# Four graph layers on one core: half-steps of a Householder reduction moved between the low halves of a software pipeline

## The chip, the core and the metric

One core of a Trainium2 chip runs the whole program as one launch. The metric is the device time in microseconds of that core, as the median of 3 runs. The engines are TensorE (PE), VectorE (DVE), ScalarE (ACT), GpSimd (POOL) and SyncE (SP), which issues the loads and stores here.

## What is computed

Four residual layers over x of shape (128, 64, 256), each `x = layernorm(x + layer(x))`. The change lies in the first one and in a small matrix job for the last one:

```python
# layer 0: two graph convolutions, then four window LSTMs (p = 1..4)
h = relu(einsum('ts,bsh->bth', adj, x @ Wg0 + bg0))
h = relu(einsum('ts,bsh->bth', adj, h @ Wg1 + bg1))
for p in range(1, 5):
    wins = h[:, :nw * p, :].reshape(Bv * nw, p, Hd)
    last = lstm_last(Wih[p-1], Whh[p-1], bih[p-1], bhh[p-1], wins)
    h = h.at[:, arange(nw) * p + (p - 1), :].set(last)
...
# layer 3: eigenvectors of the normalized 64 x 64 graph Laplacian
_, U = eigh(L_norm)
out = U @ ((U.T @ x) @ W1 ...) @ W2 ...
```

All products are made from two parts, a high half rounded to the matmul type and a low half that is the rest, with three matmuls for one (high by high, high by low, low by high: lines 473 to 475). ScalarE makes the high halves, VectorE the low ones.

## The kernel before

The 8192 rows are worked in 16 groups of 512. `graph_layers` runs them through a software pipeline of turns (`for it in range(...)`, 19 turns from 0 to 18), written out by hand for each engine; engines meet only by semaphores. In turn `it` TensorE's queue holds: `project_input(it)` (x times Wg0, 28 matmuls), `project_output(it - 2)` (times Wg1), the LSTM products of window length 1 for the second half of group `it - 3`, `mix_to_features(it - 1)` (adjacency, 24 matmuls), `mix_rows(it)` (adjacency, 6 matmuls), and the LSTM products for the first half of group `it - 2`. Products of one half are 18 matmuls of 128x512.

The results go through three pairs of PSUM banks: `pair_a` holds the projected input (`ps_y`) and the mixed features (`ps_ax`), `pair_b` the first layer and the output, `pair_c` is used by group 1's projected input alone, in turn 1; from turn 2 on its banks are part of the LSTM's ring of four.

VectorE's queue in a common turn (3 to 15) is: `hidden` of the LSTM (`hT`, L1977, waits for ScalarE's tanh), a reflection, `projected_low` (`y_lo`, L1565), `input_low` (`xs_lo`, L1561), `rows_low` (`l_x_lo`, L1910, twice), `cell` (`l_cell`, L1970), a second reflection, `mixed_low` (`ax_lo`, L1573), `first_low` (`h_lo`, L1569), `hidden`, `cell`.

A reflection is one of 62 steps of the Householder reduction of the Laplacian to tridiagonal form, on 32 partitions. Step k has three parts on VectorE: `back_products` (L206 to L214, waits for GpSimd's `scaled`), `back_update` (L222 to L231) and `front` of step k + 1 (L174 to L180). GpSimd does `basis` (L244, L246) after the update and `scalars` (L189 to L197) after the front; L196 releases the next `back_products`. So the reflections are a chain between VectorE and GpSimd that runs beside the graph stage. `REFLECTION_AT` says which halves of which turns hold one: both halves of turns 2 to 15 and the first half of 16, 29 in all. The other 33 are done in the LSTM stage of window lengths 2 and 3.

A pipeline turn's dependencies that matter here: `project_input(g)` waits for `xs_lo` of g and, from group 2 on, for `ax_lo` of g - 2 (same banks); `mix_to_features(g)` waits for `h_lo` of g and `y_lo` of g + 1 (the banks of `ps_y` are overwritten); `mix_rows(g)` for `y_lo` of g; `project_output(g)` for `ax_lo` of g and `h_lo` of g + 1; the LSTM's first-half products for `l_x_lo`.

SyncE issues the loads at the start: x of group 0, the adjacency twice in both orientations (block diagonal), Wg0, Wg1, the biases, then x of the further groups and the LSTM's first weights. `l_w1x_lo` (L1618) is the low half of those weights, in turn 1.

## Time and profile before

| | us |
|---|---|
| median of 3 runs | 2044.53 |
| lowest, highest | 2042.39, 2045.41 |
| the profiled execution | 2044.89 |
| its span in the trace | 2043.1 |
| graph stage and first LSTM, to the first product of window length 2 | 344.84 |
| turn 3's first product, turn 16's first | 55.87, 310.47 |

In the timeline a row is the start, the duration, the engine and line, what it writes and reads, and in brackets the idle time of the engine before it with what ended it.

### The profile page before, as it was taken

Reading aid. Unit: us, or ns where it says so; the run is one execution under the profiler, and the core shown is the slowest. Engines: PE = TensorE matmul, PEld = TensorE weight load, DVE = VectorE, ACT = ScalarE, POOL = GpSimd, SP = SyncE. Lnnn points to the kernel's source line nnn.
Section 4 is the critical chain, followed back from the end, with each engine's and each line's share of the span. In section 5 each row is a group of like instructions: output and inputs, shape, how many; then the busy total and the mean of one; then the engine's idle time right before and its main releaser. Section 6 shows DMA issues by size and latency. Waiting matters only on the chain. (4 is left out here: it accounts for less than half of the span.)

```text
span 2043.1 us, 32231 instructions
## 1 busy us (share of the span) xinstructions
PE 1915.3 (94%) x11545; PEld 1616.9 (79%) x11545; DVE 1519.5 (74%) x4011; ACT 1152.8 (56%) x1803; POOL 712.2 (35%) x1676
## 2 busy tenths in 40 slices
PE   6999999999999999999999989989699899689996
PEld 5888887888899999987887778867599434479895
DVE  6888786657566777888888879868565588789575
ACT  3555556445445454544344367657576688557575
POOL 2566651233233341000000056466543000108675
PEclk8999999999999999999999989989799999899898
DMA  3010101001000000010000043113212000003022
GB/s 115 22 32 22 52 1 42 1 1 42 1 1 1 1 1 1 1 42 1 1 1 1 1 150 104 63 38 97 73 65 71 1 1 1 11 30 128 22 73 83
DMA packets 61534, 71.13 MB, mean 35 GB/s; under 512 B 3767, under 2 KB 55102, under 8 KB 61374
## 3 DMA queue, kind: packets, MB, share of 16 engines
q1 hardware_dynamic: 61374, 69.07, 10.4%
q8 instruction: 91, 1.49, 0.3%
q14 instruction: 69, 0.57, 0.1%
HBM read 43.90 MB, written 25.17 MB: 34 GB/s over the span
## 5 line engine op out<-in xcount | busy, mean ns | idle before, releaser
L2002 ACT ACTIVATE l_gates<-l_acc,l_b 128x512 f32<-128x512 f32 (+1 forms) x408 | 240.7, 620 | 88.3 <-PE l_acc L475 86.3
L1900 ACT ACTIVATE l_x_hi<-hT 128x512 fp32r<-128x512 f32 (+1 forms) x144 | 101.2, 754 | 171.4 <-PE l_acc L475 170.9
L473 PE MATMUL l_acc<-l_x_hi,l_w1x_hi 128*128 128x336 f32 (+1 forms) x544 | 187.9, 345 | 4.0 <-ACT l_gates L2002 2.7
L475 PE MATMUL l_acc<-l_x_lo,l_w1x_hi 128*128 128x336 f32 (+1 forms) x544 | 188.3, 346 | 0.0
L474 PE MATMUL l_acc<-l_x_hi,l_w1x_lo 128*128 128x336 f32 (+1 forms) x544 | 188.3, 346 | 0.0
L473 PE MATMUL l_acc<-l_x_hi,l_w0x_hi 128*128 128x512 f32 x464 | 182.2, 393 | 5.4 <-ACT l_gates L2002 4.5
L475 PE MATMUL l_acc<-l_x_lo,l_w0x_hi 128*128 128x512 f32 x464 | 181.5, 391 | 0.0
L474 PE MATMUL l_acc<-l_x_hi,l_w0x_lo 128*128 128x512 f32 x464 | 181.3, 391 | 0.0
L2009 ACT ACTIVATE l_gates<-l_cell 128x512 f32<-128x512 f32 (+1 forms) x112 | 63.8, 569 | 191.2 <-DVE l_cell L2061 155.7
L244 POOL TENSOR_TENSOR bi_shifted<-bi_shifted 32x126 f32<-32x126 f32 (+61 forms) x62 | 17.7, 286 | 378.2 <-DVE bi_shifted L231 378.2
L1247 ACT ACTIVATE leaky<-sc_g 128x1024 f32<-128x1024 f32 x128 | 121.2, 1032 | 21.7 <-PE sc_g L1361 21.4
L473 PE MATMUL l_acc<-l_h_hi,l_w0h_hi 128*128 128x512 f32 x320 | 124.9, 390 | 4.4 <-DVE l_h_lo L2073 4.4
L2189 POOL TENSOR_TENSOR n_tmp<-n_stats 128x4 f32<-128x4 f32 x64 | 13.3, 208 | 329.2 <-DVE n_stats L2177 328.1
L475 PE MATMUL l_acc<-l_h_lo,l_w0h_hi 128*128 128x512 f32 x320 | 124.7, 390 | 0.0
L474 PE MATMUL l_acc<-l_h_hi,l_w0h_lo 128*128 128x512 f32 x320 | 124.7, 390 | 0.0
L473 PEld LDWEIGHTS l_acc<-l_x_hi,l_w1x_hi 128*128 128x128 f32 x544 | 103.3, 190 | 13.3 <-ACT l_gates L2002 3.2
L2206 ACT ACTIVATE hT<-hT,n_shift,n_rstd 128x256 f32<-128x256 f32 x192 | 99.4, 591 | 21.4 <-POOL n_shift L2201 21.4
L474 PEld LDWEIGHTS l_acc<-l_x_hi,l_w1x_lo 128*128 128x128 f32 x544 | 103.0, 189 | 8.6
L475 PEld LDWEIGHTS l_acc<-l_x_lo,l_w1x_hi 128*128 128x128 f32 x544 | 102.9, 189 | 8.7
L473 PEld LDWEIGHTS l_acc<-l_x_hi,l_w0x_hi 128*128 128x128 f32 x464 | 87.6, 189 | 25.5 <-ACT l_gates L2002 6.1
L2058 DVE TENSOR_TENSOR l_gates<-l_gates 128x512 f32<-128x512 f32 (+1 forms) x72 | 43.9, 610 | 80.6 <-ACT l_gates L2002 79.0
L475 PEld LDWEIGHTS l_acc<-l_x_lo,l_w0x_hi 128*128 128x128 f32 x464 | 87.4, 188 | 18.3
(519 smaller groups left out, 6231.3 us busy)
## 6 DMA issues: line engine op xcount, KB each, us to landing
xin<-in_x_t SPq DMA_DIRECT2D x16, 512.0 KB, 3.7
hidB<-in_x SPq DMA_DIRECT2D x16, 512.0 KB, 4.8
x<-hT SPq DMA_DIRECT2D x16, 512.0 KB, 3.2
hidB<-x SPq DMA_DIRECT2D x16, 512.0 KB, 3.8
x<-hidB SPq DMA_DIRECT2D x16, 512.0 KB, 2.9
attention_residual<-x SPq DMA_DIRECT2D x16, 512.0 KB, 3.9
out_x<-hT SPq DMA_DIRECT2D x16, 512.0 KB, 2.9
l_rawx<-in_wih SPq DMA_DIRECT2D x4, 1024.0 KB, 5.4
```

Of the source, the lines that this page charges most:

```text
L244: s.after(g.tensor_tensor(prod, vb[:, lo:].unsqueeze(1).to_broadcast([self.Q, 2, w]), self.p[k % 2][:, 2:4].unsqueeze(2).to_broadcast([sel ...
L473: t.matmul(out, left[0], right[0], start=start, stop=False)
L474: t.matmul(out, left[1], right[0], start=False, stop=False)
L475: return t.matmul(out, left[0], right[1], start=False, stop=stop)
L1247: a.activation(leaky[b % RING][:, :, :], ps_g[b % GATHERS][:, :, :], ACT.Prelu, alpha=SLOPE).then_inc(leaked, 1)
L1900: i = nc.scalar.activation(as_windows(xs[s % 2][0][:, ch, 0:bg * nw], nw), cols(p, bg, nw, group, k, ch), ACT.Copy)
L2002: i = a.activation(gates[:, j, q, 0:n], acc[:, j, q, 0:n], FUNC[q], bias=b[:, o:o + 1])
L2009: a.activation(tcell[:, j, 0:n], cell[:, j, 0:n], TANH).then_inc(tc, 1)
L2058: v.tensor_tensor(i_, i_, g_, ALU.mult)
L2189: s.add(p.tensor_tensor(apart, even[:, :, 1], odd[:, :, 1], ALU.subtract))
L2206: i = a.activation(rows[:, r, :], rows[:, r, :], ACT.Identity, bias=self.shift[:, g, r:r + 1], scale=self.rstd[:, g, r:r + 1])
```

## The change

- Loads: Wg0 is issued second, right behind x of group 0; Wg1 goes behind the biases. Each has a semaphore of its own, and ScalarE waits for each where it copies it.
- Start of TensorE: `project_input(0)` waits only for Wg0's low half, and for the bias's low half ahead of its first bias product.
- Banks: group 2's projected input goes to `pair_c` too, so `project_input(2)` waits for `y_lo` of group 1, and `mix_to_features(1)` no longer waits for `y_lo` of group 2.
- Reflections: in turn 2 there is only one, behind `input_low(3)` and ahead of `rows_low(0)`. In the common turns the second one is split: `mixed_low` stands between its products and its update with the next front. In turn 16 the one reflection moves from the first half to the second, behind `rows_low(14)`. 28 in all, so 34 are left to the LSTM stage.
- The wait for all reads of the ring moves from ahead of window length 2's products to their second half (`j == 1`), whose banks they are.

```diff
--- before.py
+++ after.py
@@ -478,7 +478,7 @@
 BIAS_ROWS = 96
 BEHIND = 3
 
-REFLECTION_AT = {at: k for k, at in enumerate([(it, half) for it in range(2, 16) for half in range(2)] + [(16, 0)])}
+REFLECTION_AT = {at: k for k, at in enumerate([(2, 0)] + [(it, half) for it in range(3, 16) for half in range(2)] + [(16, 1)])}
 XBUFS = 4
 
 
@@ -1411,10 +1411,10 @@
             return pair.rearrange("p c (h d) -> p (c h) d", d=D)
 
         def ps_y(g):
-            return as_rows(pair_c if g == 1 else pair_a)
+            return as_rows(pair_c if g in (1, 2) else pair_a)
         ps_h1, ps_ax, ps_out = as_rows(pair_b), pair_a, pair_b
         ps_sums = acc[:, 1, 0, 0:P]
-        w_in, x_in, b_in = sem("g_w_in"), sem("g_x_in"), sem("g_b_in")
+        w0_in, w1_in, x_in, b_in = sem("g_w0_in"), sem("g_w1_in"), sem("g_x_in"), sem("g_b_in")
         l_in, l_hi, l_lo = sem("g_l_in"), sem("g_l_hi"), sem("g_l_lo")
         hi_w, lo_w, sums, sums_done, cleared = sem("g_w_hi"), sem("g_w_lo"), sem("g_sums"), sem("g_sums_done"), sem("g_cleared")
         xh, xl, p1, yh, yl, m1, h1h, h1l, m2, axh, axl, p2, out = (sem("g_" + n) for n in (
@@ -1429,16 +1429,16 @@
 
         def on_sync(sp):
             sp.dma_start(xin[0][:, :, :], xv[0]).then_inc(x_in, 16)
+            sp.dma_start(raw[:, 0], wg0.rearrange("(c p) n -> p c n", p=P)).then_inc(w0_in, 16)
             for h in HALVES:
                 sp.dma_start(c["adj_t2"][h, h], adj_t_in).then_inc(loaded, 16)
             for h in HALVES:
                 sp.dma_start(c["adj2"][h, h], adj_in).then_inc(adj_loaded, 16)
-            sp.dma_start(raw[:, 0], wg0.rearrange("(c p) n -> p c n", p=P)).then_inc(w_in, 16)
-            sp.dma_start(raw[:, 1], wg1.rearrange("(c p) n -> p c n", p=P)).then_inc(w_in, 16)
             sp.wait_ge(cleared, 2)
             sp.dma_start(b0r[0:1, :], bg0).then_inc(b_in, 16)
             sp.dma_start(b1r[0:1, :], bg1).then_inc(b_in, 16)
             sp.dma_start(b1r[64:65, :], bg1).then_inc(b_in, 16)
+            sp.dma_start(raw[:, 1], wg1.rearrange("(c p) n -> p c n", p=P)).then_inc(w1_in, 16)
             for g in range(1, GROUPS):
                 sp.wait_ge(x_in, g * 16)
                 if g >= XBUFS:
@@ -1498,7 +1498,7 @@
                     i = a.activation(group_of(hT, g)[:, ch], ps_out[:, ch], ACT.Relu)
                 i.then_inc(out, 1)
             input_high(0)
-            act.wait_ge(w_in, 32)
+            act.wait_ge(w0_in, 16)
             a.activation(w0[0][:, :, :], raw[:, 0], ACT.Copy).then_inc(hi_w, 1)
             act.wait_ge(off, 4)
             act.wait_ge(loaded, 32)
@@ -1515,6 +1515,7 @@
             projected_high(0)
             input_high(1)
             first_high(0)
+            act.wait_ge(w1_in, 16)
             a.activation(w1[0][:, :, :], raw[:, 1], ACT.Copy).then_inc(hi_w, 1)
             for it in range(1, TURNS):
                 early, late = it - 2, it - BEHIND
@@ -1572,9 +1573,12 @@
                 dve.wait_ge(axh, g + 1)
                 v.tensor_tensor(ax[1][:, :, :], ps_ax, ax[0][:, :, :].bitcast(F32), ALU.subtract).then_inc(axl, 1)
 
-            def reflection(at):
+            def reflection_products(at):
                 if at in REFLECTION_AT:
                     hh.back_products(v, dve, REFLECTION_AT[at])
+
+            def reflection_update(at):
+                if at in REFLECTION_AT:
                     hh.back_update(v, REFLECTION_AT[at])
                     hh.front(v, dve, REFLECTION_AT[at] + 1)
             input_low(0)
@@ -1603,7 +1607,9 @@
                     lstm.weights_low(dve, it - GROUPS)
                 if late >= 0:
                     lstm.hidden(dve, late, 0)
-                reflection((it, 0))
+                if it > 2:
+                    reflection_products((it, 0))
+                    reflection_update((it, 0))
                 if it < GROUPS:
                     projected_low(it)
                 if it + 1 < GROUPS:
@@ -1618,13 +1624,17 @@
                     v.tensor_tensor(lw.split[1][:, :, :], lw.raw[:, :, :], lw.split[0][:, :, :].bitcast(F32),
                                     ALU.subtract).then_inc(l_lo, 1)
                     continue
+                if it == 2:
+                    reflection_products((it, 0))
+                    reflection_update((it, 0))
                 if early < GROUPS:
                     lstm.rows_low(dve, early)
                 if late >= 0:
                     lstm.cell(dve, late, 1)
-                reflection((it, 1))
+                reflection_products((it, 1))
                 if it - 1 < GROUPS:
                     mixed_low(it - 1)
+                reflection_update((it, 1))
                 if it < GROUPS:
                     first_low(it)
                 if late >= 0:
@@ -1644,14 +1654,18 @@
 
             def project_input(g):
                 pe.wait_ge(xl, g + 1)
-                if g >= 2:
+                if g >= 3:
                     pe.wait_ge(axl, g - 1)
+                elif g == 2:
+                    pe.wait_ge(yl, 2)
                 if g == 0:
-                    pe.wait_ge(lo_w, 2)
+                    pe.wait_ge(lo_w, 1)
                 for r in range(TILES):
                     for k in range(C):
                         n = slice(r * P, (r + 1) * P)
                         product(t, ps_y(g)[:, r], (xs[0][:, k, n], xs[1][:, k, n]), (w0[0][:, k], w0[1][:, k]), k == 0, False)
+                    if g == 0 and r == 0:
+                        pe.wait_ge(lo_w, 2)
                     i = t.matmul(ps_y(g)[:, r], ones[:, :], b0[:, :], start=False, stop=True)
                 i.then_inc(p1, 1)
 
@@ -1669,7 +1683,7 @@
 
             def mix_to_features(g):
                 pe.wait_ge(h1l, g + 1)
-                if 1 <= g < GROUPS - 1:
+                if 2 <= g < GROUPS - 1:
                     pe.wait_ge(yl, g + 2)
                 elif g:
                     pe.wait_ge(axl, g)
@@ -1838,7 +1852,6 @@
                     pe.wait_ge(w_lo, 2 * p - 3)
                 if p == 2:
                     pe.wait_ge(rows_done, GROUPS)
-                    pe.wait_ge(ring_read, 6 * GROUPS)
 
             def body(p, bg, nw, group, step, gate, split):
                 n = bg * nw
@@ -1858,6 +1871,8 @@
                             pe.wait_ge(gates_read, (step + k) * 2 + j - 1 - BEGIN)
                         if j == 0:
                             pe.wait_ge(x_lo, step + k + 1)
+                        elif step + k == GROUPS:
+                            pe.wait_ge(ring_read, 6 * GROUPS)
                         for q in used(k):
                             if late and q == FORGET:
                                 continue
```

VectorE around the start of turn 2, before (names are output <- inputs; `bi_shifted`, `bi_other` and `bi_chain` are the reflection's memory):

```order
L1617 TENSOR_TENSOR l_b<-l_b 128x32
L1618 TENSOR_TENSOR l_w1x_lo<-l_rawx,l_w1x_hi 128x2048
L206 RECIPROCAL bi_shifted<-bi_shifted 32x1
L208 TENSOR_TENSOR bi_shifted<-bi_shifted 32x4x63
L210 TENSOR_SCALAR bi_shifted<-bi_shifted 32x1
L211 TENSOR_REDUCE bi_shifted<-bi_shifted 32x4
```

and with the change:

```order
L1623 TENSOR_TENSOR l_b<-l_b 128x32
L1624 TENSOR_TENSOR l_w1x_lo<-l_rawx,l_w1x_hi 128x2048
L1566 TENSOR_TENSOR y_lo<-l_acc,y_hi 128x1024
L1562 TENSOR_TENSOR xs_lo<-xin,xs_hi 128x1024
L206 RECIPROCAL bi_shifted<-bi_shifted 32x1
L208 TENSOR_TENSOR bi_shifted<-bi_shifted 32x4x63
```

The low halves `y_lo` and `xs_lo` stood behind the whole of reflection 0 and now stand ahead of it.

VectorE in a common turn (3), the end of the second reflection, before:

```order
L179 TENSOR_SCALAR bi_shifted<-bi_shifted 32x1
L180 TENSOR_SCALAR bi_shifted<-bi_shifted 32x1
L1573 TENSOR_TENSOR ax_lo<-l_acc,ax_hi 128x1024
L1569 SCALAR_TENSOR_TENSOR h_lo<-l_acc,h_hi 128x1024
L1977 TENSOR_TENSOR hT<-l_gates 128x512
L1970 TENSOR_TENSOR l_cell<-l_gates 128x512
L1977 TENSOR_TENSOR hT<-l_gates 128x512
L206 RECIPROCAL bi_shifted<-bi_shifted 32x1
```

With the change, its middle (turn 3):

```order
L214 ISA bi_shifted<-bi_shifted,bi_other 32x61
L214 ISA bi_shifted 32x1
L1574 TENSOR_TENSOR ax_lo<-l_acc,ax_hi 128x1024
L222 TENSOR_SCALAR bi_shifted<-bi_shifted 32x1
L223 STREAM_TRANSPOSE bi_shifted<-bi_shifted 32x64
L224 SCALAR_TENSOR_TENSOR bi_chain<-bi_shifted,bi_other 32x61
```

and its end:

```order
L179 TENSOR_SCALAR bi_shifted<-bi_shifted 32x1
L180 TENSOR_SCALAR bi_shifted<-bi_shifted 32x1
L1570 SCALAR_TENSOR_TENSOR h_lo<-l_acc,h_hi 128x1024
L1992 TENSOR_TENSOR hT<-l_gates 128x512
L1985 TENSOR_TENSOR l_cell<-l_gates 128x512
L1992 TENSOR_TENSOR hT<-l_gates 128x512
L206 RECIPROCAL bi_shifted<-bi_shifted 32x1
```

`ax_lo` moved from behind the front (L178 to L180) to ahead of L222, the first operation of the update; behind the front stands `h_lo` at once.

## Rows read from the trace of the kernel before

**Rows 1.** The page, its part 1: busy time of each engine, share, instructions.
```profile
PE 1915.3 (94%) x11545; PEld 1616.9 (79%) x11545; DVE 1519.5 (74%) x4011; ACT 1152.8 (56%) x1803; POOL 712.2 (35%) x1676
```

**Rows 2.** The windows view: stretch, its length, each engine's busy us, TensorE clock, DMA.
```profile
55.87:310.47 254.60, 249.99 (x1405) 214.89 (x1404) 209.63 (x701) 147.99 (x208) 150.19 (x283) 1.00 0.08 26
310.47:344.84 34.37, 32.08 (x143) 25.96 (x142) 20.39 (x43) 23.67 (x35) 7.14 (x15) 0.95 0.18 62
344.84:2043.10 1698.26, 1595.94 (x9813) 1342.87 (x9813) 1255.23 (x3171) 958.38 (x1531) 537.43 (x1329) 0.97 0.10 33
42.11:52.35 10.24, 9.05 (x33) 8.27 (x34) 7.86 (x27) 2.02 (x2) 6.20 (x12) 0.50 0.18 51
322.00:325.41 3.41, 3.41 (x8) 2.73 (x9) 1.80 (x3) 1.94 (x3) 2.83 (x9) 0.50 0.00 0
```

**Rows 3.** The waits of TensorE from 0 to 345 us: total, times, longest.
```profile
PE l_acc L473 <- DVE y_lo L1565: 8.6, 2, 6.3
PE l_acc L473 <- DVE ax_lo L1573: 5.9, 10, 1.4
...
PE l_acc L473 <- DVE l_x_lo L1910: 1.3, 1, 1.3
```

**Rows 4.** The timeline of the start: start us, us, engine, line, what [idle before].
```profile
3.73 0.59 SPq L1436 DMA_DIRECT2D g_raw<-in_wg  x1
...
5.63 1.22 DVE L1561 TENSOR_TENSOR xs_lo<-xin,xs_hi 128x1024 fp32r<-128x1024 f32 x1 [3.52 <-ACT xs_hi L1473]
...
8.03 0.69 DVE L1582 TENSOR_TENSOR wg_lo<-g_raw,wg_hi 128x512 fp32r<-128x512 f32 x1 [1.18 <-ACT wg_hi L1502]
...
9.31 0.56 PE L473 MATMUL l_acc<-wg_hi,xs_hi 128*128 128x256 f32 x1 [3.52 <-DVE bg0r L1584]
```

**Rows 5.** The timeline of turn 2.
```profile
32.16 2.27 DVE L1618 TENSOR_TENSOR l_w1x_lo<-l_rawx,l_w1x_hi 128x2048 fp32r<-128x2048 f32 x1
...
32.25 2.32 POOL L189 TENSOR_SCALAR bi_shifted<-bi_shifted 32x1 f32<-32x1 f32 x1 [19.51 <-DVE bi_shifted L180]
...
37.32 0.15 DVE L206 RECIPROCAL bi_shifted<-bi_shifted 32x1 f32<-32x1 f32 x1 [2.88 <-POOL bi_shifted L196]
...
41.95 1.20 DVE L1565 TENSOR_TENSOR y_lo<-l_acc,y_hi 128x1024 fp32r<-128x1024 f32 x1
...
43.30 0.44 PE L473 MATMUL l_acc<-adjr_hi,h_hi 128*128 128x128 f32 x1 [6.25 <-DVE y_lo L1565]
...
44.21 1.27 DVE L1910 TENSOR_TENSOR l_x_lo<-hT,l_x_hi 128x512 fp32r<-128x512 f32 x2
...
51.12 0.63 PE L473 MATMUL l_acc<-l_x_hi,l_w1x_hi 128*128 128x512 f32 x1
```

**Rows 6.** The timeline of turns 5 and 6, VectorE and GpSimd.
```profile
108.37 0.15 DVE L206 RECIPROCAL bi_shifted<-bi_shifted 32x1 f32<-32x1 f32 x1 [2.00 <-POOL bi_shifted L196]
...
112.85 1.20 DVE L1573 TENSOR_TENSOR ax_lo<-l_acc,ax_hi 128x1024 fp32r<-128x1024 f32 x1
...
113.98 1.20 DVE L1569 SCALAR_TENSOR_TENSOR h_lo<-l_acc,h_hi 128x1024 fp32r<-128x1024 f32 x1
...
115.02 1.50 POOL L194 TENSOR_SCALAR bi_shifted<-bi_shifted 32x1 f32<-32x1 f32 x1
...
117.03 0.18 POOL L196 TENSOR_TENSOR bi_shifted<-bi_shifted 32x1 f32<-32x1 f32 x1
...
117.15 0.69 DVE L1977 TENSOR_TENSOR hT<-l_gates 128x512 f32<-128x512 f32 x1 [0.77 <-ACT l_gates L1966]
...
117.76 0.14 DVE L206 RECIPROCAL bi_shifted<-bi_shifted 32x1 f32<-32x1 f32 x1
```

**Rows 7.** The timeline of turns 15 and 16 and of the stage behind.
```profile
294.95 0.14 DVE L206 RECIPROCAL bi_shifted<-bi_shifted 32x1 f32<-32x1 f32 x1
...
321.99 0.80 PE L473 MATMUL l_acc<-l_x_hi,l_w1x_hi 128*128 128x512 f32 x1 [1.31 <-DVE l_x_lo L1910]
...
344.84 0.47 PE L473 MATMUL l_acc<-l_x_hi,l_w0x_hi 128*128 128x512 f32 x1 [0.98 <-ACT l_gates L1961]
```

## The prediction

> **What bounds the kernel now.** I read the page first, then the windows by stage, then the waits, then the timelines of the places that the diff touches. TensorE is busy 94% of the span, VectorE 74%, GpSimd 35% [rows 1]. Behind 344.84 us lies a stretch of 1698.26 us, of which TensorE is busy 1595.94 [rows 2]; the change moves only one reflection into it. All else happens ahead of 344.84, so the sum is made there.
>
> In the graph stage proper, turns 3 to 15 (55.87 to 310.47), 254.60 us hold 249.99 of TensorE work [rows 2]. That looks bound by TensorE, but it nearly isn't. The waits say that TensorE stands 5.9 us in 10 waits for `ax_lo` of VectorE [rows 3]; the mean turn is 254.60 / 13 = 19.58 us against 249.99 / 13 = 19.23 of work. What sets that small excess is a loop that holds no TensorE work: a reflection's `front` on VectorE, its `scalars` on GpSimd, the next reflection on VectorE, twice in a turn. In it VectorE waits 2.00 us for GpSimd ahead of a turn's second reflection (108.37) and not at all ahead of the first one (117.76, which follows `hT` of 117.15 at once) [rows 6]. But there GpSimd is finished (L196: 117.03 + 0.18 = 117.21) only 0.55 us before it is wanted. That 0.55 us is all the slack there is, and the prediction turns on it.
>
> Outside the common turns the losses are single: 6.25 us ahead of 43.30 in turn 2, followed by 10.24 us at granted clock 0.50, the lower level of 1.2 GHz (42.11 to 52.35); 1.31 us at 321.99, where the clock is again 0.50 for 3.41 us; 0.98 us at 344.84 [rows 2, 5, 7].
>
> **The start: -2.6 us.** The load of Wg0 is issued at 3.73, and will be second in the queue, at about 1.2 (the first issue's place plus its 0.5). TensorE begins at 9.31, and waited for `bg0r`, the bias's low half; that wait moves behind the first six products. The first start is then `xs_lo`'s end, 5.63 + 1.22, plus `wg_lo`'s 0.69, or 7.5: 1.8 us earlier [rows 4]. Those 28 products ran mostly at the lower clock; beginning earlier, they should see the full clock earlier too, which I put at 0.8 us (bounds: 0, and 1.7, half of the 3.41 us of a slow stretch [rows 2]). If Wg0 shared the queue so badly with the 512 KB ahead of it that it landed as late as now, the gain would be 0; if both terms are whole, 3.5. I take 2.6. The load of Wg1 moves behind the three bias loads; its only reader is in turn 1, so it costs nothing, and if it were late it could cost at most the 0.6 us of one issue. VectorE runs without a break from there to 34.4, so its work shifts by the same 2.6.
>
> **Turn 2: -5.6 us more.** Now VectorE waits 2.88 us for GpSimd, does reflection 0 (37.32 to 41.95, 4.6 us), and only then the low halves on which TensorE waits [rows 5]. After: `l_w1x_lo` ends at 34.4 - 2.6 = 31.8, `y_lo` and `xs_lo` at 1.13 us spacing [rows 6] end at 34.1. GpSimd's scalars took 2.9 us after 34.4; they now get 1.1 us beside `y_lo`, stand while `xs_lo` runs (below), and end 1.8 later: 35.9. Reflection 0 ends at 40.5, `l_x_lo` (1.27) at 41.8, and there the first LSTM products can start, instead of at 51.12 [rows 5]. TensorE has done its other work of the turn by then: it was free at 43.30 - 6.25 = 37.05, will be 2.6 + 1.4 sooner (group 2 has its own bank pair and no longer waits 1.4 for `ax_lo` [rows 3]), and needs half of 43.30 to 51.12 at the full clock, so it is through at 37.0. The 1.4 lies beside the reflection and counts for nothing. The products took 51.12 to 55.87, of which 1.23 us was at half rate, so 4.1 at full. I add 1.7 for one slow stretch of 3.41 us, since TensorE idles 4.8 us ahead of them (bounds 0 and 3.4: none, or two). Turn 3 starts at 41.8 + 4.1 + 1.7 = 47.6 instead of 55.87: -8.2 with the start's 2.6 inside.
>
> **The common turns: +15.6 us.** `mixed_low` (`ax_lo`, 1.13 us of VectorE's time) now stands inside the second reflection, so its `front` ends 1.13 us later and GpSimd's scalars begin 1.13 later. TensorE gets `ax_lo` sooner, but the loop is longer. From the `front`'s end at 112.85 to L196's end at 117.21 GpSimd needed 4.36 us. Of these 1.27 went to the two VectorE operations between `h_lo` and the wait for the tanh (`hT` and `l_cell`, 113.98 + 1.13 = 115.11 to 117.15 - 0.77 = 116.38): L194 takes 1.50 us across them, and L189 took 2.32 beside `l_w1x_lo`'s 2.27 [rows 5, 6]. So GpSimd's own part is 3.1 us. `ax_lo` and `h_lo`, which read a bank, do not hold it. After the change only `h_lo` (1.13) stands before `hT`, so the chain is still open when the turn's next `hT` (0.69) comes, and is held by that as well: 3.1 + 1.27 + 0.69 = 5.1 us. Before, the reflection began 117.76 - 112.85 = 4.9 after the `front`'s end. The loop grows by 1.13 + 5.1 - 4.9 = 1.3 us. There are 12 such legs between the first reflection of turn 3 and that of turn 15 (294.95) [rows 7]: 15.6 us. The least it can be is 1.13 - 0.55 = 0.6 a turn, 7.2 in all, if the last `hT` holds nothing; nothing but a gain of TensorE's could make it negative, and TensorE is not in the loop. The most is 1.5 a turn, 18. I take 1.3, as L194's row is the nearest.
>
> The Trainium skill (SBUF — State Buffer, section "Who interferes with whom") says that a VectorE instruction with two SBUF inputs contends with a GpSimd one that reads SBUF, and that whichever is issued first keeps the port while the other blocks. L194 began 0.09 us before `hT` and was held all the same (1.50 us) [rows 6]. By the page's order rule it would have run through, each leg would be about 0.13 us shorter, and the sum 1.6 us lower. The row shows otherwise, and the sum goes by the row.
>
> In turns of 20.9 us TensorE has 19.2 of work and stands about 1.7 for `y_lo`, now its latest input, ahead of the adjacency products. I add 0.7 us for slow stretches there and in turn 2 beyond the one counted; each costs 1.7 (322.00 to 325.41 at 0.50 [rows 2]), mostly inside the 1.7 of idle time.
>
> **The end of the stage: -4.0 us.** The last reflection here moves from ahead of `l_x_lo` of group 14 to behind it: the wait of 1.31 us at 321.99 goes, and with it the slow stretch that follows, 1.7. The wait for all reads of the ring (0.98 at 344.84) moves to the second half of the products, and is over by then [rows 2, 7]. Late next is nothing: `ax_lo` of group 15 is due only behind group 14's first LSTM products, and stands ahead of that reflection's update.
>
> **The rest: 0.** One reflection of 29 goes to the LSTM stage (28 remain). The one that ends up last has the shortest vectors of all, so less than reflection 0's 4.6 us of VectorE [rows 5], in a stretch where VectorE is busy 1255.23 of 1698.26 us [rows 2]. That idle time is its cover; were it gone, the price is under 4.6.
>
> **Sum.** -8.2 + 15.6 + 0.7 - 4.0 = +4.1 on the profiled execution's 2044.89, so 2049.0. The median shown, 2044.53, is 0.36 below that execution: 2048.6. A difference of 0.2%, 4.1 us, is about what a measurement can tell from none.
>
> **The rivals.**
> - *The scalars still fit (faster), 0.12.* GpSimd is held only by what lies wholly inside it, and the loop grows by 0.6 a turn. Point of decision: L196 less than 0.1 us into the turn's second `hT`. Then 8.4 less, and no slow stretches: 2039.5. For it: L196 passed beside `hT` at 117.15 unharmed. Against: L194's 1.50.
> - *The loop doesn't grow, 0.06.* `ax_lo` fills waits inside the reflection, and TensorE sets the turn: 15.6 and 0.7 less, near 2032. Against: a reflection (37.32 to 41.95) is VectorE work from end to end, with no hole of 1.13 us.
> - *The clock makes TensorE the bound, 0.15.* Idle time now lies ahead of the adjacency products, where a slow stretch lasted 10.24 us after 43.30 [rows 2]. Such a stretch costs 5.1 and the turn's idle time covers 1.7: 3.4 a time, two times in the stage give +7: 2055.5. Against: the common turns' waits of (5.9 - 1.4) / 9 = 0.5 us each left the clock at 1.00 [rows 2, 3]. The Trainium skill (TensorE: Matmul & The Clock Gate, Part 1) has the array fall to half rate after idling and rise with activity, which speaks for this rival.
> - *The new order of loads doesn't bring the start forward, 0.08.* Then 2.6 more: 2051.2.
>
> **How the numbers follow.** The forecast's own case has 0.59, with a range of 2045 to 2052 from its bounds (loop 1.1 to 1.5 a turn, clock in turn 2). A good two fifths of it lie above 2048.6. Slower: 0.24 + 0.15 + 0.07 = 0.46; same: the other 0.35 and 0.01; faster: 0.18. The range 2039 to 2056 leaves out the second rival and the ends of the third.
>
> **What would show it.** Right: first product near 7.5; turn 3 near 47.6; turn starts 20.9 apart with TensorE waiting 1 to 2 us for `y_lo`, none for `ax_lo`; L206 of each first reflection waiting about 1.2 for L196; L193 or L194 held twice. Wrong: turns at 19.6 or less, or first reflections that follow `hT` at once.

## The result and the profile after

The change takes 2051.24 us (median of 6 runs, 2050.59 to 2052.44) against 2044.3 for the kernel before (6 runs): a ratio of 1.0035, 95% interval 1.0023 to 1.0048. It is slower, by 6.9 us, a third of a per cent and clear of the noise; forecast were +4.1 and a range up to 2056. The profiled execution took 2050.59, its span is 2048.8 against 2043.1. The two spans are compared below. Two executions far out of line, one of unsplit (8814.00 us) and one of the kernel before beside it (4833.44), are left out of every median and ratio below.

The first line of the page on the change, the busy times: TensorE has 2.1 us more than in [rows 1], of a span that is 5.7 longer, so most of the loss is waiting.

```profile
PE 1917.4 (94%) x11545; PEld 1618.1 (79%) x11545; DVE 1520.9 (74%) x4011; ACT 1149.7 (56%) x1803; POOL 711.8 (35%) x1676
```

The windows view of the change, one row each for turns 3 to 15, the end of the graph stage, the rest, and two slow stretches (stretches at the lower clock, 0.50); the columns are those of [rows 2].

```profile
49.44:316.47 267.03, 254.84 (x1405) 218.52 (x1404) 210.31 (x701) 146.36 (x208) 147.38 (x280) 0.98 0.08 25
316.47:348.08 31.61, 30.39 (x142) 24.93 (x143) 20.34 (x43) 22.08 (x32) 10.67 (x18) 1.00 0.19 67
348.08:2048.80 1700.72, 1597.05 (x9814) 1343.29 (x9812) 1259.84 (x3194) 958.49 (x1532) 540.24 (x1340) 0.97 0.10 33
40.94:47.77 6.83, 4.75 (x11) 3.85 (x12) 4.12 (x9) 1.76 (x2) 4.22 (x11) 0.50 0.00 0
102.38:105.79 3.41, 3.41 (x11) 2.73 (x11) 1.35 (x6) 1.75 (x3) 2.27 (x7) 0.50 0.40 129
```

Against [rows 2] the stages stand so:

| us | before | change | difference | forecast |
|---|---|---|---|---|
| to turn 3's first product | 55.87 | 49.44 | -6.4 | -8.2 |
| turns 3 to 15 | 254.60 | 267.03 | +12.4 | +16.3 |
| end of the stage | 34.37 | 31.61 | -2.8 | -4.0 |
| the rest | 1698.26 | 1700.72 | +2.5 | 0 |
| sum | | | +5.7 | +4.1 |

TensorE's waits up to the first product of window length 2 (what waited, what it waited for: total us, times, longest). `ax_lo`, 5.9 us in [rows 3], is gone; `y_lo` stands in its place, 9 times, most of them in common turns.

```profile
PE l_acc L473 <- DVE y_lo L1566: 12.6, 9, 2.4
PE l_acc L473 <- DVE l_x_lo L1925: 6.2, 2, 5.0
...
PE l_acc L473 <- DVE h_lo L1570: 1.8, 1, 1.8
PE l_acc L473 <- DVE wg_lo L1586: 1.0, 1, 1.0
```

The timeline of TensorE at the start, in turn 2, at the end of the stage and at window length 4's first product. The first product is 1.61 us sooner than in [rows 4], turn 2's LSTM products 8.1 sooner than in [rows 5].

```profile
7.70 0.55 PE L473 MATMUL l_acc<-wg_hi,xs_hi 128*128 128x256 f32 x1 [1.03 <-DVE wg_lo L1586]
...
18.36 0.42 PE L473 MATMUL l_acc<-wg_hi,xs_hi 128*128 128x256 f32 x1
...
43.02 0.77 PE L473 MATMUL l_acc<-l_x_hi,l_w1x_hi 128*128 128x512 f32 x1 [5.03 <-DVE l_x_lo L1925]
...
316.47 0.47 PE L473 MATMUL l_acc<-ax_hi,wg_hi 128*128 128x512 f32 x1 [1.76 <-DVE h_lo L1570]
...
339.60 0.51 PE L473 MATMUL l_acc<-l_x_hi,l_w1x_hi 128*128 128x512 f32 x1 [1.22 <-DVE l_x_lo L1925]
...
885.90 0.50 PE L473 MATMUL l_acc<-l_x_hi,l_w0x_hi 128*128 128x512 f32 x1 [2.17 <-ACT l_gates L2017]
```

The timeline of VectorE and GpSimd in one common turn, from its second reflection to the next turn's first; it answers to [rows 6].

```profile
104.62 0.15 DVE L206 RECIPROCAL bi_shifted<-bi_shifted 32x1 f32<-32x1 f32 x1 [1.99 <-POOL bi_shifted L196]
...
106.31 1.23 DVE L1574 TENSOR_TENSOR ax_lo<-l_acc,ax_hi 128x1024 fp32r<-128x1024 f32 x1
...
110.27 1.20 DVE L1570 SCALAR_TENSOR_TENSOR h_lo<-l_acc,h_hi 128x1024 fp32r<-128x1024 f32 x1
111.40 0.67 DVE L1992 TENSOR_TENSOR hT<-l_gates 128x512 f32<-128x512 f32 x1
112.00 0.67 DVE L1985 TENSOR_TENSOR l_cell<-l_gates 128x512 f32<-128x512 f32 x1
113.44 0.69 DVE L1992 TENSOR_TENSOR hT<-l_gates 128x512 f32<-128x512 f32 x1 [0.77 <-ACT l_gates L1981]
114.98 0.15 DVE L206 RECIPROCAL bi_shifted<-bi_shifted 32x1 f32<-32x1 f32 x1 [0.85 <-POOL bi_shifted L196]
...
110.67 0.54 POOL L190 TENSOR_TENSOR bi_shifted<-bi_shifted 32x1 f32<-32x1 f32 x1
111.32 1.57 POOL L191 TENSOR_SCALAR bi_shifted<-bi_shifted 32x1 f32<-32x1 f32 x1
112.98 0.18 POOL L192 TENSOR_SCALAR bi_shifted<-bi_shifted 32x1 f32<-32x1 f32 x1
113.26 0.33 POOL L193 TENSOR_SCALAR bi_shifted<-bi_shifted 32x1 f32<-32x1 f32 x1
113.69 0.57 POOL L194 TENSOR_SCALAR bi_shifted<-bi_shifted 32x1 f32<-32x1 f32 x1
114.36 0.33 POOL L195 TENSOR_SCALAR bi_shifted<-bi_shifted 32x1 f32<-32x1 f32 x1
114.77 0.18 POOL L196 TENSOR_TENSOR bi_shifted<-bi_shifted 32x1 f32<-32x1 f32 x1
```

The first reflection (114.98) now waits 0.85 us for L196. In [rows 6] it followed `hT` with no gap. From the second reflection's start to the operation behind its front are 5.65 us (4.48 before, so +1.17: `ax_lo`'s slot); from there to the next reflection 4.71 (4.91 before, so -0.20). The loop has grown by 0.97 us here.

### The profile page after: what moved, and what is told of

The parts are those of the page before. It is cut to its first block and busy times, and to the rows that moved or that the text cites. A ratio compares the mean times of both kernels' runs of the same rounds, so it can differ in the third digit from the quotient of the medians.

```text
span 2048.8 us, 32245 instructions
## 1 busy us (share of the span) xinstructions
PE 1917.4 (94%) x11545; PEld 1618.1 (79%) x11545; DVE 1520.9 (74%) x4011; ACT 1149.7 (56%) x1803; POOL 711.8 (35%) x1676
## 3 DMA queue, kind: packets, MB, share of 16 engines
q1 hardware_dynamic: 61374, 69.07, 10.6%
## 5 line engine op out<-in xcount | busy, mean ns | idle before, releaser
L244 POOL TENSOR_TENSOR bi_shifted<-bi_shifted 32x126 f32<-32x126 f32 (+61 forms) x62 | 18.0, 290 | 395.7 <-DVE bi_shifted L231 395.7
```

## The experiments

The stages of all kernels, from their profiled executions (us), with the medians and ratios of their timed runs. "Refl." is the number of reflections in the graph stage; those behind it are 62 less that number.

| kernel | refl. | turn 3 at | turns 3-15 | end | rest | median | ratio (95%) |
|---|---|---|---|---|---|---|---|
| before | 29 | 55.87 | 254.6 | 34.4 | 1698.3 | 2044 | 1 |
| change | 28 | 49.44 | 267.0 | 31.6 | 1700.7 | 2051.2 | 1.0035 (1.0023-1.0048) |
| unsplit | 28 | 47.44 | 255.1 | 30.2 | 1702.9 | 2039.4 | 0.9977 (0.9966-0.9987) |
| split_only | 29 | 55.34 | 266.9 | 34.7 | 1698.9 | 2057.4 | 1.0063 (1.0047-1.0079) |
| xs_inside | 28 | 48.98 | 249.1 | 30.2 | 1697.3 | 2030.6 | 0.9937 (0.9919-0.9955) |
| after_29 | 29 | 49.22 | 267.1 | 31.6 | 1700.0 | 2048.8 | 1.0025 (1.0016-1.0035) |
| start_only | 29 | 52.53 | 254.5 | 34.3 | 1698.0 | 2042.4 | 0.9993 (0.9984-1.0003) |
| turn2_only | 28 | 50.37 | 255.0 | 34.4 | 1702.7 | 2044.0 | 0.9998 (0.9989-1.0007) |
| tail_only | 29 | 55.15 | 254.6 | 30.1 | 1698.4 | 2040.5 | 0.9982 (0.9972-0.9991) |
| xs_in_29 | 29 | 48.28 | 249.1 | 30.2 | 1698.7 | 2028.3 | 0.992 (0.9905-0.9935) |
| drop_one | 28 | 55.70 | 254.7 | 31.3 | 1701.5 | 2045.8 | 1.0008 (0.9999-1.0017) |
| tail_30 | 30 | 53.73 | 254.6 | 30.2 | 1701.9 | 2043.8 | 0.9998 (0.9989-1.0007) |
| xs_in_30 | 30 | 48.94 | 249.5 | 35.5 | 1697.0 | 2034.4 | 0.9953 (0.9936-0.9969) |

### The split: taken out of the change, and put alone into the kernel before

**unsplit** is the change with its second reflection in one piece again:

```diff
                 reflection_products((it, 1))
+                reflection_update((it, 1))
                 if it - 1 < GROUPS:
                     mixed_low(it - 1)
-                reflection_update((it, 1))
```

> The changed kernel with the common turns' second reflection in one piece again (the low half of the mixed features behind it); loads, banks, turn 2 and turn 16 stay as changed. Theory 1 (the loop of VectorE and GpSimd got longer because the low half stands inside it): turns 3 to 15 take 254 to 256 us instead of 267.0, VectorE no longer waits 0.85 us for GpSimd ahead of a turn's first reflection, TensorE waits for ax_lo again, and the time is 2051.2 - 12 = 2039, between 2037 and 2042. Rival (the slow clock stretches in the common turns, or the new order of turn 2, made the loss): turns 3 to 15 stay above 262 us and the time above 2047.

Measured 2039.4 us, 11.8 below the change, with turns 3 to 15 at 255.11. The timeline of VectorE, and then the waits of TensorE, show the old picture: the first reflection follows `hT` at once, and TensorE waits for `ax_lo`.

```profile
109.02 0.69 DVE L1992 TENSOR_TENSOR hT<-l_gates 128x512 f32<-128x512 f32 x1 [0.77 <-ACT l_gates L1981]
109.63 0.14 DVE L206 RECIPROCAL bi_shifted<-bi_shifted 32x1 f32<-32x1 f32 x1
```

```profile
PE l_acc L473 <- DVE ax_lo L1574: 5.2, 10, 0.9
```

**split_only** is the kernel before with the opposite edit, in turns 2 to 15.

> The kernel before with the split alone: the low half of the mixed features stands between products and update of the second reflection in turns 2 to 15, and nothing else is changed. Theory 1: +1.0 us a turn as in the changed kernel, so 2044.3 + 12.4 = 2056.7, between 2054 and 2059, with a wait of 0.85 us for GpSimd ahead of each first reflection. Rival (the split is harmless by itself, and costs only together with the new places of turn 2 and 16): 2044 to 2046.

Measured 2057.35 us. Turns 3 to 15 take 266.92, as in the change, and the same 0.85 us stands ahead of each first reflection, here on VectorE's timeline:

```profile
119.55 0.69 DVE L1982 TENSOR_TENSOR hT<-l_gates 128x512 f32<-128x512 f32 x1 [0.77 <-ACT l_gates L1971]
121.09 0.15 DVE L206 RECIPROCAL bi_shifted<-bi_shifted 32x1 f32<-32x1 f32 x1 [0.85 <-POOL bi_shifted L196]
```

What follows: the split costs 12 us in these turns with or without the other edits. The loop between VectorE and GpSimd sets them, and the clock doesn't: split_only has 17.1 us of slow stretches in these turns and 257.75 us of TensorE work, the change 10.2 and 254.84, and both take 267 us.

### Another low half inside the reflection

**xs_inside** has `ax_lo` behind the reflection as before, and puts the next group's `xs_lo` (same length, but two inputs in SBUF where `ax_lo` reads one from a bank) between the products and the update, in turns 3 to 14:

```diff
-                if it + 1 < GROUPS:
+                if it + 1 < GROUPS and it < 3:
                     input_low(it + 1)
...
                 reflection_products((it, 1))
+                if 3 <= it < GROUPS - 1:
+                    input_low(it + 1)
+                reflection_update((it, 1))
                 if it - 1 < GROUPS:
                     mixed_low(it - 1)
-                reflection_update((it, 1))
```

> The changed kernel, but in turns 3 to 14 it is the low half of the next group's input (xs_lo, two SBUF inputs) that stands inside the second reflection, taken from behind the first one; the low half of the mixed features stands behind the reflection again. Theory 2 (GpSimd's scalars are held while VectorE works on two SBUF inputs): behind the first reflection there is then 1.13 us less of holding work, VectorE still waits 2.0 us for GpSimd, the leg from the first reflection to the second is 1.13 us shorter and the one back 1.13 us longer: turns as in the unsplit kernel, 19.6 us, and 2038 to 2042. Rival (the scalars take their 5.8 us there by themselves, whatever VectorE does): the leg to the second reflection stays, VectorE waits 3.1 us there, each turn is 1.1 us longer, and the time is 2051 to 2054.

Measured 2030.62 us, better than either theory said and better than both kernels. In the windows view TensorE is busy 248.59 of the 249.09 us of these turns:

```profile
48.98:298.07 249.09, 248.59 (x1406) 214.80 (x1405) 210.77 (x701) 146.88 (x207) 130.94 (x283) 1.00 0.08 26
```

Its timeline between the first and the second reflection of a turn, VectorE and then GpSimd, and last GpSimd's L191 in such a leg of the kernel before:

```profile
191.68 1.20 DVE L1566 TENSOR_TENSOR y_lo<-l_acc,y_hi 128x1024 fp32r<-128x1024 f32 x1
192.91 1.29 DVE L1927 TENSOR_TENSOR l_x_lo<-hT,l_x_hi 128x512 fp32r<-128x512 f32 x2
194.12 0.69 DVE L1987 TENSOR_TENSOR l_cell<-l_gates 128x512 f32<-128x512 f32 x1
196.02 0.15 DVE L206 RECIPROCAL bi_shifted<-bi_shifted 32x1 f32<-32x1 f32 x1 [1.21 <-POOL bi_shifted L196]
...
192.72 0.33 POOL L191 TENSOR_SCALAR bi_shifted<-bi_shifted 32x1 f32<-32x1 f32 x1
193.14 0.51 POOL L192 TENSOR_SCALAR bi_shifted<-bi_shifted 32x1 f32<-32x1 f32 x1
193.75 1.19 POOL L193 TENSOR_SCALAR bi_shifted<-bi_shifted 32x1 f32<-32x1 f32 x1
```

```profile
182.86 3.31 POOL L191 TENSOR_SCALAR bi_shifted<-bi_shifted 32x1 f32<-32x1 f32 x1
```

GpSimd is held 0.33 us in L192 (0.51 against 0.18) and 0.86 in L193 (1.19 against 0.33), 1.19 in all. Before, `xs_lo` too stood in this leg, and one run of two-input operations, `xs_lo`, `l_x_lo` twice and `l_cell`, held L191 from 182.86 on: it took 3.31 instead of 0.33, 2.98 more. The wait ahead of the second reflection was 2.00 [rows 6]; now it is 1.21. The leg from the first reflection to the second shrinks from 10.5 us to 8.7, by 1.8: not by `xs_lo`'s 1.13 but by what GpSimd is held less, 2.98 - 1.19 = 1.79. The leg back grows from 9.3 to 10.5. The turn is 19.1 us instead of 19.6 and its loop has slack again. Inside a reflection GpSimd waits for VectorE between two of its jobs (4.13 us ahead of L244 in this run), so an operation that would hold it costs nothing there but its own 1.13. That the two moves differ by 18 us in these turns (249.1 against 267.0) is shown; that `xs_lo` wins because GpSimd is held less is shown by the rows of this one leg, and no run separates it further.

### The start, turn 2 and the end, each alone in the kernel before

**start_only** has the new loads, the two semaphores and the later wait for `bg0r`:

```diff
             sp.dma_start(xin[0][:, :, :], xv[0]).then_inc(x_in, 16)
+            sp.dma_start(raw[:, 0], wg0.rearrange("(c p) n -> p c n", p=P)).then_inc(w0_in, 16)
...
                 if g == 0:
-                    pe.wait_ge(lo_w, 2)
+                    pe.wait_ge(lo_w, 1)
```

> The kernel before with the new order of loads, the two semaphores and the later wait for the bias's low half, and nothing else. Theory 1, the start is worth its 1.8 us and little more: first product at 7.7 to 7.9, turn 1 at 18.3 to 18.5 (before 20.00), and those 1.6 us reach turn 3 (about 54.2 instead of 55.87); median 2042 to 2043, ratio near 0.9992. Theory 2, the prediction's: the clock also rises earlier, so turn 1 comes 2.6 us sooner (17.4) and the median is 2041.5. Rival: VectorE's chain with GpSimd in turn 2 takes the gain back, turn 3 stays at 55.5 or later and the median at 2044.

Measured 2042.41 us, 1.7 below the kernel before; the interval takes in 1. TensorE's timeline has the first product at 7.86:

```profile
7.86 0.55 PE L473 MATMUL l_acc<-wg_hi,xs_hi 128*128 128x256 f32 x1 [1.09 <-DVE wg_lo L1583]
```

In this profiled execution turn 1 begins at 16.83, 3.2 us sooner than before; in the change it begins 1.64 sooner (20.00, 18.36). The clock makes the difference. Before, it rose at 14.81 and fell back from 18.22 to 21.63; in the change it rose at 13.63 and fell back from 17.04 to 20.46; in start_only the products quicken at 11.2 already and show no fall ahead of turn 1. unsplit, whose start is the change's, has its first reflection at 35.34 where the change has it at 36.97, 1.63 sooner. So one and the same start differs by some 1.5 us between executions. The edit gives 1.6 us with the clock of before and no more, which is also the difference of the medians (1.7); the interval takes in 1, so that the median alone doesn't show it.

**turn2_only** has `REFLECTION_AT` without (2, 1), the reflection of turn 2 behind `input_low(3)`, and the spare banks for group 2:

```diff
-                reflection((it, 0))
+                if it > 2:
+                    reflection((it, 0))
...
+                if it == 2:
+                    reflection((it, 0))
                 if early < GROUPS:
                     lstm.rows_low(dve, early)
```

> The kernel before with turn 2 as in the change (one reflection there instead of two, behind the low half of group 3's input; the spare banks for group 2) and 28 reflections in all. Theory 1: turn 3 starts 4.5 to 5.5 us sooner than before (50.4 to 51.4), turn 1 as before at 20.0, the common turns keep 254.6, and the rest behind the first product of window length 2 grows from 1698.2 by 1 to 3 us for the 34th reflection; median 2040.5 to 2042.5. Theory 2, the bounds of the prediction: without the start's part it is 5.6, and the rest stays: 2038.5 to 2039.5. Rival: the idle time ahead of the LSTM products lowers the clock over the next stretch too, and turn 3 comes at 52.5 or later.

Turn 3 starts 5.5 us sooner (forecast for this term: 5.6), with TensorE's wait in turn 2 as in the change:

```profile
44.57 0.62 PE L473 MATMUL l_acc<-l_x_hi,l_w1x_hi 128*128 128x512 f32 x1 [5.09 <-DVE l_x_lo L1915]
```

Yet the median is 2044.02, as before: the rest has grown by 4.5 us. The expectation had 1 to 3. Of the 4.5 us TensorE is busy 2.9 (1598.83 against 1595.94), with the same products, so a part of the growth is slow clock and not the 34th reflection.

**tail_only** has (16, 1) for (16, 0) and the wait for the ring's reads at the second half:

```diff
-                    pe.wait_ge(ring_read, 6 * GROUPS)
...
                         if j == 0:
                             pe.wait_ge(x_lo, step + k + 1)
+                        elif step + k == GROUPS:
+                            pe.wait_ge(ring_read, 6 * GROUPS)
```

> The kernel before with the last reflection in the second half of turn 16 and the wait for the ring's reads at the second half of the products; 29 reflections as before. The prediction's theory: the wait of 1.31 us and the slow stretch behind it go, and the 0.98 at the first product of window length 2: that product comes 4.0 us sooner after turn 16's first one (30.4 instead of 34.37); median near 2040. Theory 2, by the trace of the change (31.61): a wait for the low halves in the last turns takes 1.2 us back, so 31.6 and a median of 2041.3. Rival: the reflection only moves the wait to the next products, 34 us as before, median 2044.

Measured 2040.52 us, 3.6 below. The windows view has TensorE busy from end to end of this stretch, 4.2 us shorter than in [rows 2]:

```profile
309.73:339.87 30.14, 30.14 (x143) 24.84 (x142) 20.03 (x43) 22.69 (x33) 5.96 (x15) 1.00 0.21 71
```

The change has 31.61 there, unsplit 30.17. What is missing in the change is the split's doing: it leaves VectorE late, and TensorE waits 1.22 us for `l_x_lo` at 339.60. The wait of 1.76 for `h_lo` at 316.47 has the same cause but ends where this stretch begins, so it is part of turns 3 to 15.

### The rest: how many reflections are left to the LSTM stage

**after_29** is the change with a 29th reflection, in the second half of turn 17:

```diff
-REFLECTION_AT = {at: k for k, at in enumerate([(2, 0)] + [(it, half) for it in range(3, 16) for half in range(2)] + [(16, 1)])}
+REFLECTION_AT = {at: k for k, at in enumerate([(2, 0)] + [(it, half) for it in range(3, 16) for half in range(2)] + [(16, 1), (17, 1)])}
```

> The changed kernel with a 29th reflection in the graph stage, in the second half of turn 17, so that the LSTM stage has 33 as before. Theory 3 (the 34th reflection makes VectorE late in the last steps of window length 3 and in those of length 4): the stretch behind the first product of window length 2 is 1698.3 us again instead of 1700.7, and the time 2048.8, between 2047.5 and 2050. Rival (that stretch differs only by where the slow clock stretches fell): 2050.5 to 2052, or the same stretch of 1700.7.

Measured 2048.84 us, 2.4 below the change. The profiled rest was only 0.7 shorter (1700.0; it has a slow stretch at 736.55 that the change lacks), so this run alone settles little.

**drop_one** is the kernel before with the reflection of turn 16 left out of the graph stage:

```diff
-REFLECTION_AT = {at: k for k, at in enumerate([(it, half) for it in range(2, 16) for half in range(2)] + [(16, 0)])}
+REFLECTION_AT = {at: k for k, at in enumerate([(it, half) for it in range(2, 16) for half in range(2)])}
```

> The kernel before without the reflection of turn 16, so 28 in the graph stage and 34 behind it, all else as before. Theory 1 (the 34th reflection of the LSTM stage costs VectorE time at the end of window length 3 that nothing hides): the rest behind the first product of window length 2 grows by 2.0 us at the end of window length 3 (about 1700.3 to 1702, against 1698.2 and 1698.4 with 29), as in the four other kernels with 28. Its graph stage ends 3 to 4 us sooner, since the wait of 1.31 at 321.99 and the slow stretch behind it go: median 2041.5 to 2043.5. Theory 2, the prediction's (its cover hides it): rest 1698.2 to 1699, median near 2040.5. Rival to theory 1: what the four kernels share is the spare banks or turn 2's order, and the rest here stays as before.

The rest is 1701.5, as theory 1 expected; the median, 2045.84, is above what it gave (2043.5 at most). VectorE's timeline near the end of window length 3 and TensorE's first product of window length 4, of the kernel before:

```profile
786.84 0.14 DVE L206 RECIPROCAL bi_shifted<-bi_shifted 32x1 f32<-32x1 f32 x1
...
793.72 0.51 DVE L2058 TENSOR_TENSOR l_gates<-l_gates 128x336 f32<-128x336 f32 x1 [4.64 <-ACT l_gates L2002]
...
797.34 0.50 DVE L2058 TENSOR_TENSOR l_gates<-l_gates 128x336 f32<-128x336 f32 x1
...
880.98 0.50 PE L473 MATMUL l_acc<-l_x_hi,l_w0x_hi 128*128 128x512 f32 x1 [1.15 <-ACT l_gates L2002]
```

and of drop_one, with one more row of TensorE:

```profile
783.68 0.14 DVE L206 RECIPROCAL bi_shifted<-bi_shifted 32x1 f32<-32x1 f32 x1
...
794.08 0.14 DVE L206 RECIPROCAL bi_shifted<-bi_shifted 32x1 f32<-32x1 f32 x1
...
795.18 0.51 DVE L2058 TENSOR_TENSOR l_gates<-l_gates 128x336 f32<-128x336 f32 x1
...
822.74 0.39 PE L473 MATMUL l_acc<-l_h_hi,l_w1h_hi 128*128 128x336 f32 x1 [0.68 <-DVE l_h_lo L2073]
...
879.74 0.50 PE L473 MATMUL l_acc<-l_x_hi,l_w0x_hi 128*128 128x512 f32 x1 [2.16 <-ACT l_gates L2002]
```

The idle time is there: after the 33rd reflection (786.84) VectorE waits 4.64 us for ScalarE. But the 34th doesn't stand in it. It stands at 794.08, one LSTM step further, ahead of an L2058 that in the kernel before follows without a wait. Counted from window length 2's first product, that L2058 begins at 797.34 - 344.84 = 452.50 us before and at 795.18 - 341.67 = 453.51 in drop_one, 1.0 us late, and the work behind the reduction follows one LSTM step later. TensorE feels it twice: it waits 0.68 us for `l_h_lo` at 822.74, where it has no wait before, and 2.16 instead of 1.15 at window length 4's first product. That product comes 880.98 - 344.84 = 536.14 us behind window length 2's before, and 879.74 - 341.67 = 538.07 in drop_one: +1.9. In the change it is 885.90 - 348.08 = 537.82: +1.7. In split_only and after_29, which have 29 reflections, both extra waits are missing; their product comes 0.8 and 0.7 us late by one slow stretch each (744.19, 736.55).

So a 34th reflection costs 1.7 to 1.9 us in the two kernels whose rows show it. The whole rests differ by more than that, since the slow stretches fall elsewhere from one execution to the next: they are 105.2 us of the rest before, 108.7 in the change and in split_only, 109.0 in drop_one. That is one stretch of 3.41 us, worth 1.7, between the kernel before and each of the others. xs_inside is the odd one in the table: 28 reflections and a rest of 1697.3, the second shortest. Its profiled execution was its fastest, 3.3 us below its median, and no row here says whether the two waits are missing in it.

**xs_in_29** is xs_inside with the 29th reflection in turn 17, the best of what the runs had pointed to:

> The version with the input's low half inside the second reflection (2030.6), with a 29th reflection in the second half of turn 17. Theory 1: as with the same addition to the change (2051.2 to 2048.8), the rest loses 1 to 3 us, since the 34th reflection of the LSTM stage goes and with it VectorE's work at the end of window length 3: median 2028 to 2029.5. Rival: its cost at the end of the graph stage (up to 3 us of VectorE ahead of the low halves of turn 17) takes that back: 2030 to 2032.

Measured 2028.26 us, 2.4 below xs_inside, ratio 0.992 (0.9905 to 0.9935): faster than the kernel before by 16 us. The gain over xs_inside is one of medians of four executions each; their profiled rests go the other way (1697.3, 1698.7). Its stages in the windows view, the graph stage's two bound by TensorE:

```profile
48.28:297.41 249.13, 248.65 (x1406) 214.94 (x1404) 211.03 (x701) 146.90 (x207) 131.07 (x283) 1.00 0.09 26
297.41:327.56 30.15, 30.15 (x143) 24.84 (x142) 23.03 (x64) 22.23 (x33) 10.24 (x20) 1.00 0.21 71
```

**tail_30** adds (17, 1) to tail_only, which gives 30.

> The kernel with the last reflection in the second half of turn 16 and the later wait for the ring's reads (2040.5), with a 30th reflection in the second half of turn 17. Theory 1 with a price per reflection: the rest gets 2 us shorter once more (1696.3), median 2038.5 to 2039. Theory 1 with a threshold (one unit of the LSTM stage takes 33 without a loss, and the 34th alone was too many, VectorE having idle time elsewhere): rest 1698 as with 29, median 2040 to 2041. Rival: the reflection in turn 17 delays the low halves there, the end grows from 30.1 to over 31, median over 2041.

Measured 2043.85 us, 3.3 above tail_only. Neither price nor threshold was right: the end stayed at 30.15, but the rest grew to 1701.9. With 30 reflections, work that follows them moves ahead by a step, and TensorE waits 2.04 us for `l_h_lo` at 858.37, where tail_only waits for nothing. So of 28, 29 and 30 the middle one fits this order of the queue, and the rest doesn't get shorter with each reflection taken from it. Why the work ahead of its place costs more here isn't traced further.

**xs_in_30** adds (17, 0) to xs_in_29.

> The best version so far (2028.3) with one more reflection in the first half of turn 17, 30 in all. There it stands ahead of the low halves of the last group's rows, on which TensorE waits, while the reflection of turn 17's second half stands behind them. Theory 1: 4 us of VectorE ahead of those low halves, of which 2.4 lie in waits that it has there (for the tanh), so TensorE gets them 1.5 to 3 us later and may see a slow stretch (1.7): end 31.7 to 35 against 30.15, median 2030 to 2033. Rival: a price per reflection in the rest (2 us) pays for it: 2027 to 2029.

Measured 2034.38 us, 6.1 above xs_in_29 and above what either side expected. Theory 1 had the mechanism and too small a price, as TensorE's timeline shows:

```profile
324.15 0.79 PE L473 MATMUL l_acc<-l_x_hi,l_w1x_hi 128*128 128x512 f32 x1 [3.90 <-DVE l_x_lo L1927]
```

These 3.90 us, with slow clock behind them (the next product takes 0.63 us against some 0.40), make the end 5.4 us longer.

## Why the prediction was right or wrong

- **The common turns** had the right mechanism: a loop without TensorE in it, lengthened by `ax_lo`, with GpSimd's slack of 0.55 us used up. Shown by split_only and unsplit, from both sides. The size was too large: 12 turns grew by 12.2 us, 1.02 each, not 1.3, and just below the 1.1 that bounded the forecast's own case. The term at fault is the turn's last `hT`, put at a full 0.69. GpSimd had got to L194 only 0.25 us after that `hT` began; L194 took 0.57 against some 0.26 when nothing holds it, so the hold was 0.31. The first hold came as foreseen: L191 took 1.57, 1.24 more than its 0.33 elsewhere, against 1.27.
- **The clock's +0.7** was not needed. The change has slow stretches inside the common turns (102.38 and 143.34, 10.2 us in all; TensorE's busy time there is 4.8 us longer than before), and the idle time took them up: the legs from one reflection to the next keep their length through them (10.6 and 10.3 us around 143 us, as in the turns beside it). TensorE's own turns are uneven there (19.0 to 24.1 us), 20.5 on average. The rival that had the clock make TensorE the bound didn't come about. The Trainium skill (TensorE: Matmul & The Clock Gate, Part 1) has the array fall to half rate after idling. Both stretches do follow a wait for `y_lo` (1.40 us at 99.84, 1.53 at 141.72); six other waits of 0.97 to 1.36 us in these turns had none behind them.
- **The start** gave its 1.6 us of the 1.8; the 0.8 for an earlier rise of the clock was wrong. In the change the clock rose 5.9 us behind the first product, against 5.5 before and 3.3 in start_only; when it rises differs between executions.
- **Turn 2** came out: 5.5 us alone against 5.6. In the change turn 3 begins 1.8 us later than forecast, 1.0 of it the start's shortfall, 0.6 a slow stretch of 6.83 us in place of the 3.41 assumed (the products took 43.02 to 49.44, 6.4 us, against 5.8), the other 0.2 VectorE's.
- **The end** was right alone (-4.2 against -4.0) and is -2.8 in the change. "Late next is nothing" held for the edit by itself; the terms were not independent, as the longer loop leaves `h_lo` and `l_x_lo` late in the last turns.
- **The rest: 0** is the term whose reason failed, +2.5 us. The prediction named the cover as the mean idle time of VectorE over 1698 us, 443 in all. But the reflection is issued at a fixed place in VectorE's order, and what counts is whether VectorE has room at that place: it hasn't in that step of window length 3, though it idles 4.64 us shortly before. The rows give this 1.7 us in the change and 1.9 in drop_one; what is left of the 2.5 is of the size that the slow stretches move about. In turn2_only the rest took back most of what turn 2 brought (-5.5 and +4.5), the reflection by itself less than half. The bound given, under 4.6, held.

The errors partly cancel: 1.8 and 1.2 short on the gains, 2.5 for the rest, against 3.9 too much on the common turns. That 2051.24 lies inside the 2045 to 2052 of the forecast's own case is in part luck: with the rest at 2.5 and the gains as measured, its own +16.3 for the common turns would have given some 2054 us. So the 2.6 us between forecast and median say less for the working than the table of stages does.

## What to carry to other kernels

When an operation moves into a chain that runs between two engines, write down the chain's other engine at each moment: a place where that engine waits anyway takes the work that would hold it, and a place where it works takes only what doesn't hold it. Moving fill work between two stages isn't free because the receiving engine idles on average; look at the very step where it will be issued. And a gain that is only a sum of separate terms should be checked for terms that feed each other, such as a longer loop and the slack behind it.

## What the runs showed of the hardware

- Whether a GpSimd operation is held by a VectorE one with two inputs in SBUF hangs on tenths of a microsecond. L191, begun 0.08 us ahead of `hT`, took 1.57; L194, begun 0.09 ahead in [rows 6], took 1.50; but L193 of the change, begun 0.18 ahead of the next `hT` (113.26, 113.44), and L191 of xs_inside, begun 0.19 ahead of `l_x_lo`, ran through in their 0.33. It is no chance of one turn: in the kernel before L194 was held all 13 times that it began 0.08 or 0.09 ahead of `hT`, and in the change L193 ran through all 12 times that it began 0.18 or 0.19 ahead. Between them the cases divide: L196 ran through 13 times at 0.11 or 0.12 before, L195 was held once at 0.11 in split_only. VectorE's operations took the same time in each case (`hT` 0.67 to 0.69 in both kernels). The Trainium skill (SBUF — State Buffer, "Who interferes with whom") gives the port to whichever is issued first. The cases from 0.18 on agree, those at 0.08 and 0.09 don't, at least by these start times; by when they were issued no row tells.
- A whole run of two-input operations on VectorE holds one GpSimd operation to its end: L191 took 3.31 us at 182.86 before, across `xs_lo`, `l_x_lo` and `l_cell`, 0.33 where nothing holds it.
- `h_lo` and `ax_lo`, with one input from a bank, don't hold GpSimd: L190 took 0.54 beside `h_lo` in the change (110.67) and 0.54 beside `ax_lo` before (113.25).
- In the first 20 us the clock of one and the same start differs between executions, worth some 1.5 us (turn 1 at 18.36 in the change, 18.61 in after_29 and 16.83 in start_only, all with the new loads). A difference of that size in one profiled execution is no effect of an edit.
- A wait on TensorE isn't surely followed by a slow stretch: 2.17 us at 885.90 in the change was (887.44, 3.41 us), 2.16 at 879.74 in drop_one, ahead of the same product, wasn't.
